# Where the sine product of a rotary embedding stands: behind or ahead of the transfers that swap a head's halves

## The reference, cut to what matters

```python
q = (hn @ Wq + bq).reshape(mh)
k = (hn @ Wk + bk).reshape(mh)

def _rope(x):
    d2 = x.shape[-1] // 2
    ...
    neg_half = jnp.concatenate([-x[..., d2:], x[..., :d2]], axis=-1)
    return x * cos + neg_half * sin
```

## Time and profile before

| | us |
|---|---|
| median of 3 runs | 2310.25 (2309.42 to 2313.67) |
| the profiled execution: time | 2305.9 |
| its span | 2304.1 |
| TensorE busy | 2144.3 (93%) |
| VectorE busy | 1691.7 (73%) |
| GpSimd busy | 1435.4 (62%) |
| ScalarE busy | 958.2 (42%) |

### The profile page before, as it was taken

How to read it: one execution, slowest core, us unless ns; L and a number is a source line. 1 busy time by engine, 2 the same in 40 slices (tenths; PEclk the granted TensorE clock), 3 DMA queues, 4 the chain that set the end, 5 groups by cost and what they waited for, 6 DMA issues and landing times.

```text
span 2304.1 us, 43543 instructions
## 1 busy us (share of the span) xinstructions
PE 2144.3 (93%) x15872; PEld 1407.3 (61%) x15872; DVE 1691.7 (73%) x2318; ACT 958.2 (42%) x1301; POOL 1435.4 (62%) x1204
## 2 busy tenths in 40 slices
PE   5779999999999999899999999999999999889997
PEld 4446565556565656455656565556565654789996
DVE  8567878787878787777877777787777775466654
ACT  3334444444434443434444444444344445333433
POOL 2447777777777777566868686878687779200000
PEclk8799999999999999989999999999999999899999
DMA  5100101010101011101111111111111130222200
GB/s 161 63 22 19 46 19 46 21 43 22 42 24 41 24 41 54 48 19 32 33 32 33 32 33 33 33 32 33 33 29 36 29 115 10 96 92 73 100 19 28
DMA packets 79484, 100.45 MB, mean 44 GB/s; under 512 B 13984, under 2 KB 43680, under 8 KB 79008
## 3 DMA queue, kind: packets, MB, share of 16 engines
q1 hardware_dynamic: 79264, 97.60, 14.2%
HBM read 40.93 MB, written 23.07 MB: 28 GB/s over the span
## 4 chain that ended last, share of the span: by engine, by line
PE 73%; DVE 17%; issue 6%; ACT 1%; DMA 1%; SPq 1%; POOL 1%; DVEq 0%; ACTq 0%
PE o_ps L1150 17%; PE m_ps L1098 8%; DVE mpart L748 6%; PE x_ps L1053 6%; PE s_ps L1119 4%; PE x_ps L1055 4%; PE x_ps L1054 4%; PE s_ps L1121 4%; PE s_ps L1125 4%; PE s_ps L1123 4%; PE gu_ps L1053 2%; PE gu_ps L1054 2%; PE gu_ps L1055 2%; PE x_ps L1157 1%; DVE rot L787 1%
## 5 line engine op out<-in xcount | busy, mean ns | idle before, releaser
L474 POOL TENSOR_TENSOR acc<-acc,pt 128x512 f32<-128x512 f32 (+3 forms) x1024 | 1235.4, 1238 | 232.6 <-ACT pt L533 232.0
L748 DVE TENSOR_REDUCE mpart<-m_ps 128x2 f32<-128x1024 f32 (+2 forms) x576 | 625.6, 1086 | 342.1 <-PE m_ps L1098 205.5
L533 ACT ACTIVATE pt<-s_ps 128x1024 f32<-128x1024 f32 (+3 forms) x640 | 545.1, 896 | 561.7 <-PE s_ps L1125 319.5
L1150 PE MATMUL o_ps<-pt,v 128*64 128x512 f32 (+3 forms) x2560 | 555.4, 556 | 0.0
L1098 PE MATMUL m_ps<-qk 64*128 64x512 f32 (+3 forms) x1280 | 285.8, 442 | 102.5 <-DVE mpart L748 85.1
L1098 PEld LDWEIGHTS m_ps<-qk 64*128 64x128 f32 x1280 | 121.8, 186 | 384.0 <-issue 217.3
L1150 PEld LDWEIGHTS o_ps<-pt,v 128*64 128x64 f32 x2560 | 158.5, 139 | 232.5 <-issue 211.4
L469 POOL TENSOR_TENSOR acc<-pt 128x512 f32<-128x512 f32 (+1 forms) x128 | 165.5, 1313 | 200.0 <-ACT pt L533 200.0
L1119 PE MATMUL s_ps<-qk 64*128 64x512 f32 (+3 forms) x1280 | 249.8, 385 | 0.0
L1121 PE MATMUL s_ps<-qk 64*128 64x512 f32 (+3 forms) x1280 | 235.9, 363 | 0.0
L1125 PE MATMUL s_ps<-aux,ones_r 64*128 64x512 f32 (+3 forms) x1280 | 235.8, 362 | 0.0
(11 more groups left out here) (161 smaller groups left out, 3406.7 us busy)
## 6 DMA issues: line engine op xcount, KB each, us to landing
rot<-qr SPq DMA_DIRECT2D x512, 64.0 KB, 2.0
attn<-o_n SPq DMA_DIRECT2D x64, 256.0 KB, 2.1
o_raw<-attn SPq DMA_DIRECT2D x8, 2048.0 KB, 9.0
w_raw<-in_wqkv SPq DMA_DIRECT2D x51, 128.0 KB, 2.6
h_g<-in_h SPq DMA_DIRECT2D x8, 512.0 KB, 3.6
out<-out_g SPq DMA_DIRECT2D x7, 512.0 KB, 2.9
qk_place<-in_h SPq DMA_DIRECT2D x4, 512.0 KB, 5.8
pt<-in_h SPq DMA_DIRECT2D x4, 512.0 KB, 10.6
```

The source lines that it names most:

```text
L474: nc.gpsimd.tensor_tensor(sums, sums, probs, ALU.add).then_inc(summed, 1)
L533: nc.scalar.activation(pt[:, u % SLOTS, :, q0:NB], s_ps[:, two:two + 2, q0:NB], ACT.Exp, scale=SCALE)\
L748: nc.vector.tensor_reduce(dst, m_ps[:, :, 0:w], AX.X, ALU.max, negate=True).then_inc(maxed, 1)
L1150: last = nc.tensor.matmul(o_ps[rows, q0:NB], v[par][:, j, rows], pt[:, u % SLOTS, a, q0:NB], start=(j == 0), stop=(j == n - 1), skip_group ...
```

## The change

ScalarE's eviction (`piece_raw`) is gone. VectorE now makes the sine product itself, out of PSUM and ahead of the transfers: `products` computes (projection + bias) x sin into `qr`, raises `qk_raw`, and then computes the cosine product into `qc`. SyncE swaps the halves of the finished product, and `turned_sum` only adds. Since the product is swapped after the sign has been applied, the table's sign is turned around. The wait for the biases moves from ScalarE to VectorE.

```diff
-            def piece_raw(n, c, a, par, i, first=False):
-
-                if c == 0 and a == 0:
-                    act.wait_ge(b_in, n * 32 + 32)
-                if not first:
-                    act.wait_ge(roped, n * (2 * BLOCKS) + (2 * c + a - 1))
-                act.wait_ge(qk_proj, n * (2 * BLOCKS) + (2 * c + a + 1))
-                nc.scalar.activation(qr[:, a, :], qk_bank[i][a], ACT.Identity, bias=b_qk[:, par, a:a + 1])\
-                  .then_inc(qk_raw, 1)
...
-                    if g in PIECE and kind is not LAST:
-                        piece_raw(it + 1, *PIECE[g], 1 - par, 2)
...
-            def cosine(n, c, a, par, i):
-
+            def products(n, c, a, par, i):
+
+                if c == 0 and a == 0:
+                    dve.wait_ge(b_in, n * 32 + 32)
+                dve.wait_ge(qk_proj, n * (2 * BLOCKS) + (2 * c + a + 1))
+                nc.vector.scalar_tensor_tensor(qr[:, a, :], qk_bank[i][a], b_qk[:, par, a:a + 1],
+                                               sin_sb[:, NB * c:NB * (c + 1)], ALU.add, ALU.mult).then_inc(qk_raw, 1)
                 if c >= 2 or i == 2:
                     dve.wait_ge(qk_lo, n * (2 * BLOCKS) + (2 * c + a - 3))
-                dve.wait_ge(qk_raw, n * (2 * BLOCKS) + (2 * c + a + 1))
                 nc.vector.scalar_tensor_tensor(qc[:, c % 2, a, :], qk_bank[i][a], b_qk[:, par, a:a + 1],
                                                cos_sb[:, NB * c:NB * (c + 1)], ALU.add, ALU.mult).then_inc(cos_done, 1)
 
-            def sine(n, c, a):
+            def turned_sum(n, c, a):
                 i = 2 * c + a
                 dve.wait_ge(rot_in[a][c % 2], n * (BLOCKS * 32) + 64 * (c // 2 + 1))
-                nc.vector.tensor_tensor(rot[:, a, :], rot[:, a, :], sin_sb[:, NB * c:NB * (c + 1)], ALU.mult)\
-                  .then_inc(rope_mul, 1)
-                dve.wait_ge(rope_mul, n * (2 * BLOCKS) + (i + 1))
                 dve.wait_ge(cos_done, n * (2 * BLOCKS) + (i + 1))
                 nc.vector.tensor_tensor(qc[:, c % 2, a, :], qc[:, c % 2, a, :], rot[:, a, :], ALU.add).then_inc(roped, 1)
...
-    sign = np.where(np.arange(P)[:, None] % DK < HALF, np.float32(-1), np.float32(1))
+
+    sign = np.where(np.arange(P)[:, None] % DK < HALF, np.float32(1), np.float32(-1))
```

More of the change, by code:

```diff
@@ L219, in postln_block_kernel @@
         cos_done = sem("cos_done")
-        rope_mul = sem("rope_mul")
         roped = sem("roped")
@@ L599, in next_hi @@
                   .then_inc(a_hi, 1)
-            def raw(c):
-                for a in range(2):
-                    piece_raw(0, c, a, 0, c % 2, first=(c == 0))
             def rounded(c):
@@ L616, in _ @@
             root_input(3)
-            raw(0)
             affine(4)
             affine(5)
-            raw(1)
             affine(6)
@@ L624, in _ @@
             root_input(4)
-            raw(2)
             rounded(1)
-            raw(3)
             rounded(2)
@@ L837, in pair @@
                     if g - 1 in PIECE and kind is not LAST:
-                        cosine(it + 1, *PIECE[g - 1], 1 - par, 2)
+                        products(it + 1, *PIECE[g - 1], 1 - par, 2)
                     if g - 1 in VALUES and kind is not LAST:
@@ L850, in pair @@
                     if g - 1 in PIECE and kind is not LAST:
-                        sine(it + 1, *PIECE[g - 1])
+                        turned_sum(it + 1, *PIECE[g - 1])
                     if ended is not None:
@@ L877, in unturned @@
                 for a in range(2):
-                    cosine(0, c, a, 0, c % 2)
+                    products(0, c, a, 0, c % 2)
                 values(0, c, 0, c % 2)
@@ L882, in turned @@
                 for a in range(2):
-                    sine(0, c, a)
+                    turned_sum(0, c, a)
             def remainders(c):
```

## The result

The changed kernel takes 2329.15 us (median of 4 runs, 2324.86 to 2331.31) against 2310.91 for the kernel before (4 runs, 2309.42 to 2313.67): ratio 1.0075, 95% interval 1.0056 to 1.0094. It is 0.75% slower. The forecast was 2328.5, in a range from 2312 to 2339. All times in this document are of executions at the usual granted clock (0.95 to 0.98 on average); one of the kernel before, 2391.37 us at a mean clock of 0.865, is left out.

The account below looks back on a forecast made before the run. TensorE's waits for VectorE's max reductions were taken to bound the kernel. Terms 15.0 + 3.0 - 0.6 - 2.0 + 2.8 = +18.2 us on 2305.9 gave 2324.1, plus 4.35 to the timed median: 2328.5, range 2312 to 2339.

Parts of the forecast that it names:

- The transfer's price: Swapping transfers, from product's end to use by VectorE's sum: taken as 3.84 us, with 4.4 as the other end.
- Q0 and K0: Middle pairs, first query and key pieces: a wait of 0.05 us, and 0.31 more on TensorE's 1.44 us wait.
- Q2: Middle pairs, third query piece: the maximum slips behind the added product, so TensorE, without slack, waits 0.58 us.
- Q1 and K1: Middle pairs, second query and key pieces: later sum data and slipped maxima cost TensorE 0.21 us together.
- K2, Q3, K3: Middle pairs, later pieces: VectorE is idle before the first maximum, so the second product hides; 0 us.
- Prologue: Last chunk before the pairs: transfers leave later and the key's sum waits; +3.0 us, range 0 to 4.
- Switching pair: Pair at 937 to 1009 us: ScalarE's rounding of the next batch's rows starts sooner without the evictions; -2.0 us.
- The clock: Value matmuls after the 1.44 us wait: two more middle pairs get a half-clock stretch, about 1.4 each; +2.8 us.
- The contention's price: Rival: VectorE's contention with GpSimd goes, 2297 us, if transfers land within 2.8 us of their signal; chance 0.08.
- no slack at Q2: Rival: TensorE has slack there and the prologue's wait is covered, leaving +1.4, 2311.7 us; chance 0.10.
- The rival in which the clock decides: All 13 middle pairs go through the half-clock stretch behind the first key piece: +23.8, 2334 us; chance 0.20.
- The signs: Changed profile: VectorE some 60 us waiting for transfers, maxima waits 100 us or more; wrong if a pair is under 116.

Follow-up runs that it names:

- the second product: Kernel before, with one more sine-type product ahead of each cosine product in the head pairs, overwritten by it; 2369.66 us, ratio 1.0275.
- the old prologue: Changed kernel with the prologue of before (ScalarE evicts, VectorE's sine product behind the transfers), pairs as changed; 2330.96 us, ratio 1.007.
- the swap held back: Kernel before, with SyncE's swap of the halves waiting for the cosine product instead of ScalarE's eviction; 2399.93 us, ratio 1.0401.
- without the swap: Changed kernel whose sum reads the unswapped sine product, while the transfers still run; 2285.25 us, ratio 0.989.
- the lagged sum: Changed kernel, in head pairs the sum behind the next group's first maximum and ScalarE's rounding behind that group's exponentials; 2299.46 us, ratio 0.9946.
- cosine behind: Changed kernel, with the cosine product moved behind the group's first maximum in the head pairs; 2319.65 us, ratio 1.0041.

## Why the prediction was right

**What decides.** Right. It is VectorE's queue in front of TensorE's maxima, by two mechanisms that each slowed a kernel when applied alone: the product ahead of the maxima (the second product, 1.0275) and the late transfer (1.0401 alone; 43 us back without its wait; and 90 us down to about 6 once a group lies between). The time came within 0.7 us of the forecast, and that closeness is luck: the terms below were off by more, in both directions.

**The transfer's price.** Taken as 3.84 us (each of the four lands 2.0 us behind its issue, and they are issued one by one); 3.87 to 3.92 for Q0 in ten pairs. The other end, 4.4, was too near: three pairs had 5.2 to 5.7, and they cost about 1.0 each in K0's wait, besides a longer stretch at the low clock.

**Q0 and K0, predicted 0.36 per pair.** Too large. VectorE was idle 0.99 at the sum (predicted 1.07), but the sum itself took 1.46 instead of 1.64, and from Q0's first product to K0's maximum 8.23 us passed, against 8.05. K0's wait rose by 0.08 to 0.16, not 0.31, and in three pairs by 1.0 to 1.1. And it doesn't last: by the last maximum ahead of Q2, TensorE is within 0.1 us of where it was before.

**Q1 and K1, predicted 0.21.** Wrong: in the usual pair K1 still has no wait; three pairs have one of 0.93 to 0.97 (fifth, sixth, twelfth), but the fifth and twelfth had 0.92 before too.

**Q2, predicted 0.58.** Right in place, too small in size: a wait of 0.66 to 0.70 in every pair, and 0.84 to 0.87 us of delay, nearly all of the 0.9. **K2, Q3, K3,** counted at nothing: TensorE has no new wait there, though K3's transfers too came late for the sum in six pairs (0.43 to 1.17 us).

**The sum of a pair.** 0.9 instead of 1.15, or 11.7 instead of 15.0 in 13 pairs. The total is near only because Q0, K0 and K1 (0.57 forecast, 0.1 or less left) and Q2 (0.58 forecast, some 0.85) were wrong in opposite ways; the slow transfers (3.0) fill the rest of the gap. Both are luck.

**Prologue, +3.0.** It measured +3.8 where it was placed, and was then given back in the first pair (-3.0, where I had -0.6). So the term was right at its place and wrong for the end: with the old prologue the time is the same. **Switching pair, -2.0.** It measured -0.7: TensorE's two long waits behind VectorE's split of the rows shrank from 3.87 and 3.50 us to 3.43 and 3.15. The rounding did start sooner: VectorE's waits for it fell from 2.24 and 1.74 us to 0.57 and none. But it wasn't all that TensorE waited for; at the second of the two maxima it was 1.4 us ahead, where I had 2.5, and Q2's wait took 0.7 back.

**The clock, +2.8.** Three more stretches and not two, 1.5 us each: 4.5. It is a net count: two of the seven pairs of before have none now (seventh, eleventh), and five others have one, so the longer wait doesn't tell which pair is stretched. This rests on the rows of one trace of each kernel; the granted clock was 0.79 over 1212 to 1220 and 1.00 in the same place when K0's wait was 0.64. All thirteen pairs had a wait of 1.53 us or more there, and ten the stretch; Q2's wait of 0.7 was never followed by one.

**The rivals.** The contention's price was real (the sum took 1.46 in the tenth pair and 0.79 in the fifth, where it came later), but its condition wasn't met: no transfer was seen to land within 2.8 us. TensorE had no slack at Q2. The rival in which the clock decides is a part of the result, at half its size.

**The signs.** As announced: the wait at Q2, VectorE idle 0.99 ahead of Q0's sum, 65.6 us of waiting for rot, ScalarE 87 less busy. Not as announced: K0's wait was 1.53 to 1.60 in the usual pair and not 1.8, the waits for the maxima 96.3 us and not 100 or more, and VectorE's work fell by 65 us and not 40, since the sums took 142.3 us instead of 174.3 in all. One sign of being wrong did come: a pair shorter than 116 us. Three pairs took 115.4 to 115.6. It was badly chosen, since the kernel before had a plain pair of 114.58; against that one they are longer.

## What to carry to other kernels

Before you move a product ahead of a transfer, look at what covers the transfer now: a step that stands between its signal and its use is not only cost. Where VectorE or any engine works in order, put the consumer of a transfer behind enough other work, here one group further, before you change who produces it; that gave 0.5 to 0.65%, and then it hardly mattered that the transfer left one product later. Price both sides of such an edit alone, since here each half measured far more than the change that combined them, where the old product was gone from behind the maxima.

## What was not expected of the hardware

Four transfers of 64 KB, issued one after another, usually took 3.84 to 3.92 us from the product's end to a sum that waited for them; for Q0 of three pairs 5.2 to 5.7. Why was not tested, but the traces show what ran beside them. In the middle pairs of the changed kernel 68 sums waited for rot, 14 of them 4.1 us or more behind the product's end. In 13 of these 14 a packet of the queue for instructions (q8, 16 KB) ran in the first 3.9 us behind the product's end, and in 2 of the other 54. In the kernel with the swap held back it was 20 of 21 against 6 of 69. So late transfers and this queue's packets came together; what holds the transfer, and whether the packets' place can be moved, is open.

A wait of TensorE of 1.4 to 1.6 us may or may not be followed by a stretch at half clock (3.09 and 1.72 us for the same eight matmuls, behind waits of 1.44 and 1.45). By and large longer waits had it more often. Over the 13 middle pairs of each trace, by K0's wait: 0.22 to 0.64 us, none of 26 (without the swap, and with the lagged sum); 0.99, none of six (cosine behind); 1.43 to 1.46, seven of 13 (before); 1.53 to 1.60, seven of ten (changed); 1.92 to 2.10, six of seven (cosine behind); 1.98 to 2.03, eight of 13 (second product); 2.38 to 2.57, 15 of 16 (swap held back, and the three slow pairs of the changed kernel). In these traces the granted clock over the 8 us from K0's maximum was 1.00 wherever there was no stretch and 0.80 or less wherever there was. A kernel gets more back than the wait itself: 1.5 us for each stretch that goes.
